# Interaction network of three layers: two sets of PSUM accumulators, one sum a period, and its transposes behind the first group of the next period

## What is computed

```python
hidden = x                                     # (512, 39, 32)
for i in range(3):
    z = jnp.einsum('bmd,bnd->bmnd', x, hidden).reshape(B, -1, D)
    cur = jnp.einsum('bcd,co->bod', z, Ws[i]) + bs[i][None, :, None]
    cur = jax.nn.relu(cur)
    if i != 2:
        hidden, direct = cur[:, :100, :], cur[:, 100:, :]
    else:
        direct = cur
    finals.append(direct)
result = jnp.sum(jnp.concatenate(finals, axis=1), axis=-1)
```

## Time and profile before

| | us |
|---|---|
| median of 3 runs | 2722.32 |
| lowest, highest | 2720.38, 2722.56 |
| profiled execution, its own time | 2722.41 |
| its span in the trace | 2720.6 |
| PE, DVE, ACT busy | 2661.5, 2642.0, 1668.8 |
| granted PE clock, mean | 0.996 |

### The profile page before, as it was taken

One profiled execution on the slowest core, in us unless ns is written; L12 is line 12 of the kernel. 1 busy time (PEld: TensorE's weight loads), 2 busy tenths in 40 slices (PEclk: granted clock), 3 DMA queues, 4 the chain that ended last, 5 costly groups with the idle time before them and its releaser, 6 DMA issues.

```text
span 2720.6 us, 52076 instructions
## 1 busy us (share of the span) xinstructions
PE 2661.5 (98%) x17960; PEld 2658.2 (98%) x17960; DVE 2642.0 (97%) x2728; ACT 1668.8 (61%) x2842; POOL 0.7 (0%) x7
## 2 busy tenths in 40 slices
PE   3899999999999999999999999999999999999999
PEld 3899999999999999999999999999999999999999
DVE  5999999999999999999999999999999999999998
ACT  3566666666666666666666666666666666666664
POOL 0000000000000000000000000000000000000000
PEclk9899999999999999999999999999999999999999
DMA  9554444444455444444544444444454444445442
GB/s 221 130 141 112 114 132 118 110 127 129 112 132 142 120 110 129 126 110 122 133 125 125 132 125 110 124 130 110 115 134 122 111 130 126 110 120 131 114 110 63
DMA packets 231026, 335.70 MB, mean 123 GB/s; under 512 B 28104, under 2 KB 165300, under 8 KB 230836
## 3 DMA queue, kind: packets, MB, share of 16 engines
q1 hardware_dynamic: 230934, 334.50, 47.2%
HBM read 329.71 MB, written 6.60 MB: 124 GB/s over the span
## 4 chain that ended last, share of the span: by engine, by line
PE 96%; DMA 1%; SPq 1%; DVE 1%; ACT 0%; issue 0%; DVEq 0%; ACTq 0%
PE acc L765 61%; PE acc L766 28%; PE acc L758 6%; PE turned L778 1%; DMA x_right<-x_by_unit 1%; DMA mixed<-in_L_rec_W_dram 0%; DMA z<-w_rows_again 0%; PE x_turned L787 0%; DVE w_split L388 0%; DVE z L430 0%; ACT w_split L650 0%; DVE z_low L435 0%; SPq L228 0%; DMA xb<-in_r_x_dram 0%; SPq L254 0%
## 5 line engine op out<-in xcount | busy, mean ns | idle before, releaser
L765 PE MATMUL acc<-w_split,z_high 128*128 128x400 f32 (+1 forms) x8320 | 2495.8, 367 | 48.1 <-DVE z_low L435 42.0
L766 PE MATMUL acc<-w_split,z_low 128*128 128x200 f32 (+1 forms) x8320 | 2121.6, 255 | 0.0
L765 PEld LDWEIGHTS acc<-w_split,z_high 128*128 128x128 f32 (+1 forms) x8320 | 1566.9, 188 | 50.6 <-issue 35.9
L766 PEld LDWEIGHTS acc<-w_split,z_low 128*128 128x128 f32 (+1 forms) x8320 | 1594.6, 192 | 0.0
L615 ACT ACTIVATE z_high<-z 128x1024 fp32r<-128x1024 f32 (+3 forms) x1152 | 1112.0, 975 | 702.0 <-DVE z L430 583.9
L435 DVE TENSOR_TENSOR z_low<-z,z_high 128x1024 fp32r<-128x1024 f32 (+3 forms) x1152 | 1281.7, 1113 | 29.6 <-PE acc L766 27.0
L430 DVE TENSOR_TENSOR z<-mixed,xb 128x1024 f32<-128x1024 f32 (+2 forms) x1024 | 1208.6, 1180 | 0.1
L640 ACT ACTIVATE mixed<-turned 32x128 f32<-32x128 f32 x768 | 204.5, 266 | 8.9
L758 PE MATMUL acc<-w_whole,z 128*128 128x200 f32 x1024 | 197.9, 337 | 1.4 <-DVE s L449 1.4
L758 PEld LDWEIGHTS acc<-w_whole,z 128*128 128x128 f32 x1024 | 169.4, 191 | 1.7 <-DVE s L449 1.7
L637 ACT ACTIVATE mixed<-turned 96x512 f32<-96x512 f32 x256 | 151.0, 590 | 11.0 <-PE turned L778 7.9
(11 more groups left out here) (29 smaller groups left out, 50.7 us busy)
## 6 DMA issues: line engine op xcount, KB each, us to landing
xb<-x_by_unit SPq DMA_DIRECT2D x384, 384.0 KB, 4.2
x_right<-x_by_unit SPq DMA_DIRECT2D x384, 136.5 KB
xb<-x_by_unit SPq DMA_DIRECT2D x384, 128.0 KB, 4.9
xb<-x_by_unit SPq DMA_DIRECT2D x128, 336.0 KB
xb<-x_by_unit SPq DMA_DIRECT2D x128, 84.0 KB
x_left<-x_by_unit SPq DMA_DIRECT2D x384, 19.5 KB
mixed<-in_L_rec_W_dram SPq DMA_DIRECT2D x4, 600.0 KB, 8.7
x_by_unit<-mixed SPq DMA_DIRECT2D x12, 160.0 KB, 2.8
```

The source lines that it names most:

```text
L765: nc.tensor.matmul(a[:, 0:2 * O], z_high[slot % HIGH_RING][0:rows, tok], w, start=(c == 0), stop=False, skip_group_check=True)
L766: last = nc.tensor.matmul(a[:, 0:O], z_low[slot % RING][0:rows, tok], w[:, 0:O], start=False, stop=(c == chunks - 1), skip_group_check=True)
```

## The change

There are now two sets of three accumulator banks; a period uses the set of its parity (`par = d % 2`), so no item writes a bank that the last period's sum still reads. With 6 banks for accumulators and one each for `turned` and `x_turned`, the turned input of a later tile goes through one bank in three parts, each part with its own wait (`turn_x`, `turned_x`), placed at three points of the period d = 4; for the first tile it uses the second set. The two half copies of a period become one of 600 columns, and the two sums one of 600, which stands behind the low part of item 2 of the next period, where `sums2` stood. `s` holds layer 2 in one row of both halves, so the addition into `direct` of 400 columns is now two of 200. `dup` and both hidden copies of ACT stand behind that sum, `dup` and the first of them behind the high part of item 3 instead of item 2. PE waits at the start of a period for the sum before the last one (`ended(n - 2)`), the wait ahead of item 5 is gone, and the transposes stand behind item 0 of the next period instead of behind item 8. `ident` has a tile of its own. At the start the second pass of layer 0 no longer waits for the first sum; at the end the last sums are cut into more pieces.

```diff
 def layers_ended(r, d):
-    return (1, 2) if r == TILES - 1 and d >= D - 2 else (0, 2)
+    if (r, d) == (0, 0):
+        return 0, 2
+    if r == TILES - 1 and d >= D - 2:
+        return 1, (2 if d == D - 1 else 3)
+    return 0, 3
...
-        acc = banks("acc", 3)
+        both = banks("acc", 6)
+        acc = [both[:, 0:3, :], both[:, 3:6, :]]
         turned = banks("turned", 1)
-        x_turned = banks("x_turned", X_BANKS)
+        x_turned = banks("x_turned", 1)
...
 # vector engine
-            def sums(a, b, step, added):
+            def sums(a, b, par, step, added):
                 dve.wait_ge(half_in, step)
                 if added is not None:
                     dve.wait_ge(direct_in, added)
-                nc.vector.tensor_tensor(s[:, a:b, :, 0:HID], acc[:, a:b, 0:O].rearrange("p l (h o) -> p l h o", o=HID),
+                nc.vector.tensor_tensor(s[:, a:b, :, 0:HID],
+                                        acc[par][:, a:b, 0:O].rearrange("p l (h o) -> p l h o", o=HID),
                                         half[:, a:b, :, :], ALU.add).then_inc(s_in, 1)
-            def sums2(u):
...
                 else:
-                    add(0, 4).then_inc(direct_in, 1)
+                    add(0, 2)
+                    add(2, 4).then_inc(direct_in, 1)
...
                 lows(base + 2, slot(2), P, group_chunks(2))
-                if not second:
-                    sums2(n - 2)
+                sums(last_a, last_b, 1 - par, ended(n - 1), n + 1)
...
                 lows(base + q + 2, slot(q + 2), P, group_chunks(2))
-                if not final:
-                    sums(a, b, ended(n), n + 2)
...
 # after the last period
             product12(2, UNITS - 1, 1, 0, at, at)
-            sums2(UNITS - 2)
+            dve.wait_ge(s_in, UNITS + 2)
+            dve.wait_ge(direct_in, UNITS + 1)
+            add(1, 2).then_inc(direct_in, 1)
             for g in range(1, GROUPS):
                 product12(2, UNITS - 1, 1, g, at + g, at + g)
+                if g == 1:
+                    sums(2, 3, 1, UNITS + 3, None)
...
 # scalar engine
                 highs(base + 2, slot(2), P, group_chunks(2))
+                second_half(last_a, last_b, 1 - par, base - 1)
                 if second:
                     high_piece(2, 2)
                     act.wait_ge(w_low_done, 8)
-                else:
-                    second_half2(base - 1)
+                highs(base + 3, slot(3), P, group_chunks(3))
+                dup(last_a, 2, ended(n - 1))
                 hidden(1, n - 1, 1 - par, ended(n - 1))
-                highs(base + 3, slot(3), P, group_chunks(3))
...
-                if not final:
+                if last_a == 0:
                     hidden(0, n + 1, 1 - par, ended(n - 1))
+                if turn:
+                    turned_x(r + 1, 0)
                 highs(base + q, slot(q), P, split_chunks(2, 0))
+                highs(base + q + 1, slot(q + 1), P, group_chunks(1))
                 if turn:
-                    for bank in range(X_BANKS):
-                        turned_x(r + 1, bank)
-                highs(base + q + 1, slot(q + 1), P, group_chunks(1))
+                    turned_x(r + 1, 1)
...
 # tensor engine
-                pe.wait_ge(s_in, ended(n - 1))
-                multiply(1, base, slot(0), 0)
-                multiply(1, base + 1, slot(1), 1)
+                pe.wait_ge(s_in, ended(n - 2))
+                multiply(1, par, base, slot(0), 0)
+                transpose(last_a, 2, ended(n - 1))
+                multiply(1, par, base + 1, slot(1), 1)
+                if turn:
+                    turn_x(r + 1, 0)
...
-                if not second:
-                    pe.wait_ge(s2_in, n - 1)
...
-                    multiply(2, base + q + g, slot(q + g), g)
-                if not final:
-                    transpose(a, b, ended(n))
+                    multiply(2, par, base + q + g, slot(q + g), g)
+                    if turn and g == 0:
+                        turn_x(r + 1, 2)
...
             at = first(UNITS)
-            pe.wait_ge(s2_in, UNITS - 1)
+            pe.wait_ge(s_in, UNITS + 1)
```

More of the change, by code:

```diff
@@ L467, in directs @@
                         fresh(0, 1)
[L468 removed]
+                    add(1, 2)
+                    add(2, 4).then_inc(direct_in, 1)
                 elif d == 1:
@@ L499, in _ @@
             low_piece(1, 1, 0)
-            sums(0, 1, 1, None)
+            sums(0, 1, 0, 1, None)
             low_piece(2, 1, 1)
@@ L512, in _ @@
             low_piece(3, 1, 2)
-            sums(0, 1, 2, 1)
+            sums(0, 1, 1, 2, 1)
             product12(1, 0, 0, 2, at + 2, at + 2)
@@ L574, in period @@
                 if final:
-                    sums(a, b, ended(n), n + 2)
+                    sums(a, b, par, ended(n), n + 2)
                 product12(2, n - 1, 1 - par, 3, base + q + 3, slot(q + 3))
                 lows(base + q + 2, slot(q + 2), P, group_chunks(2))
-                if not final:
-                    sums(a, b, ended(n), n + 2)
             for r in range(TILES):
@@ L615, in highs, with second_half @@
                 nc.scalar.activation(z_high[slot % HIGH_RING][0:rows, 0:n * T], z[0:rows, slot % RING, 0:n * T], ACT.Copy).then_inc(high, 1)
-            def second_half(a, b, last):
+            def second_half(a, b, par, last):
                 act.wait_ge(freed, RING + last + 1)
-                nc.scalar.activation(half[:, a:b, :, :], acc[:, a:b, O:2 * O].rearrange("p l (h o) -> p l h o", o=HID), ACT.Copy)\
+                nc.scalar.activation(half[:, a:b, :, :], acc[par][:, a:b, O:2 * O].rearrange("p l (h o) -> p l h o", o=HID), ACT.Copy)\
                   .then_inc(half_in, 1)
[L623 to L626, removed]
             def dup(a, b, step):
@@ L641, in hidden, with turned_x @@
                 last.then_inc(hid_in[l + 1], 1)
[L643 to L647, removed]
+            def turned_x(r, part):
+                n = min(X_PER_BANK, BLOCKS - X_PER_BANK * part)
+                act.wait_ge(x_turned_in, X_PARTS * r + part + 1)
+                nc.scalar.activation(xts(r)[:, X_PER_BANK * part:X_PER_BANK * part + n, :],
+                                     x_part(r, part)[:, 0:n * T].rearrange("p (k t) -> p k t", t=T), ACT.Copy).then_inc(xts_in, 1)
             def high_w(w, st):
@@ L654, in high_piece @@
                 high_w(piece(l, g), stage(l, g))
-            for bank in range(X_BANKS):
-                turned_x(0, bank)
+            for part in range(X_PARTS):
+                turned_x(0, part)
             act.wait_ge(pair_sum, 1)
@@ L723, in period @@
                     dup(a, b, ended(n))
-                else:
-                    second_half(a, b, base + q - 1)
                 highs(base + q + 3, slot(q + 3), P, group_chunks(3))
-                if not final:
-                    dup(a, b, ended(n))
+                if turn:
+                    turned_x(r + 1, 2)
             for r in range(TILES):
@@ L779, in transpose, with turn_x @@
                 last.then_inc(turned_in, 1)
-            def turn_x(r):
+            def turn_x(r, part):
                 pe.wait_ge(x_in, 32 * (r + 1))
                 if r > 0:
-                    pe.wait_ge(xts_in, X_BANKS * r)
-                for k in range(BLOCKS):
-                    bank, j = k // X_PER_BANK, k % X_PER_BANK
-                    t = nc.tensor.transpose(x_turned[:, bank, j * T:(j + 1) * T], x_tile(r)[:, k * P:(k + 1) * P], ident)
-                    if j == X_PER_BANK - 1 or k == BLOCKS - 1:
-                        t.then_inc(x_turned_in, 1)
+                    pe.wait_ge(xts_in, X_PARTS * r + part)
+                for k in range(X_PER_BANK * part, min(BLOCKS, X_PER_BANK * (part + 1))):
+                    j = k % X_PER_BANK
+                    last = nc.tensor.transpose(x_part(r, part)[:, j * T:(j + 1) * T], x_tile(r)[:, k * P:(k + 1) * P], ident)
+                last.then_inc(x_turned_in, 1)
             pe.wait_ge(consts, 2)
-            turn_x(0)
+            for part in range(X_PARTS):
+                turn_x(0, part)
             pe.wait_ge(w_low_done, 1)
-            multiply(0, 0, 0)
+            multiply(0, 0, 0, 0)
             transpose(0, 1, 1)
+            pe.wait_ge(xts_in, X_PARTS)
+            multiply(0, 1, 1, 1)
             pe.wait_ge(s_in, 1)
-            multiply(0, 1, 1)
             at = first(0)
```

88 lines of the change are left out of this document (42 added, 46 removed).

## The result

The changed kernel takes 2763.04 us (median of 4 runs, 2762.85 to 2763.98) where the kernel before took 2721.5 in the runs beside it: a ratio of 1.0154, with an interval of 1.0142 to 1.0166. The prediction was 2760, in a range of 2735 to 2788. The profiled execution has a span of 2761.1 us, 40.5 more than before.

The account below looks back on a forecast made before the run. PE was taken to set the pace, with DVE 0.2 us to spare a period. A new PE stall of 125 x 0.31 = 39 us, + 1 - 2, gave 2722.4 + 38 = 2760 us, range 2735 to 2788.

Parts of the forecast that it names:

- T0: The end of item 8's last matmul on PE, taken as zero of the clock of one period.
- Stop and restart: At the transposes: PE stands 0.27 us for `dup`, plus 0.04 for a slower restart, 0.31 us a period.
- the walk through the three slots: DVE's low parts followed from item 3's end through slot waits: low part 2 starts 0.19 us after item 8 ends.
- The bounds: Limits for PE's stall at the transposes: 0.08 and 0.50 us a period, with 0.31 taken.
- A: Rival: ScalarE's copies, within 0.1 us of need, delay low part and sum; 0.5 us a period, 2784 us; chance 0.15.
- The count: PE's stall at the transposes comes about 125 times: 125 x 0.31 = 39 us.
- At the start I took 2 us off: Layer 0's first pass: PE's later items stand closer to it; 2 us saved, between 0 and 3.
- The copies of the turned input: ACT's first copy ahead of item 5's high part at d = 4: 1 us for three periods, 0 to 2.7.
- At the end I had "nothing": Last sums: PE's 1.4 us wait shortened by 0.3, an extra addition costs 0.2; counted as nothing.
- The first tie: Hidden copy of layer 1 ends at 4.61, DVE wants it for item 5 at 4.58; few hundredths, no cost.
- B: Rival: path to `dup` is 0.27 us shorter, so the transposes are not late; 2721 us, no change; chance 0.08.
- C: Rival: DVE is the real pace, freeing its sums gives back 0.2 us a period; 2697 us; chance 0.05.

Follow-up runs that it names:

- early sum: Changed kernel with layers 0 and 1 summed behind the low part of item 1, layer 2 summed apart in the merged sum's place: 2718.96 us, ratio 0.9995 to the kernel before.
- exchanged sum: Changed kernel with two neighbouring VectorE instructions exchanged, the merged sum ahead of item 2's low part: 2718.51 us, ratio 0.9996 to the kernel before.

## Why the prediction was right

**The bound and the path.** The step that carried the forecast was that PE, without spare time, must wait for low part, sum, `dup` and transposes, all behind T0. It holds: when the path was shorter by 0.21 or longer by 0.13, the period followed; with `dup` over in time (early sum, exchanged sum) the loss is gone; with DVE's load cut it stays.

**Its pieces.** Predicted and measured, from T0: low part 0.19 and 0.21; sum 1.33 and 1.34, its length 0.78 and 0.78; end of `dup` 2.39 and 2.39; transposes 2.45 and 2.45. Stop and restart 0.27 + 0.04 against 0.26 + 0.05, the period 20.95 in both. That close, the walk through the three slots was worth its length: starting the low part at the lower bound, T0 + 0.11, would have given 0.23 and 29 us. The bounds were added up less well: with the pieces named there the lower one is 0.10 and not 0.08 (0.08 needs a sum of 0.68), the upper one 0.52 and not 0.50. Neither moves the range, which starts from 0.11 and ends in A.

**The count.** 125 times 0.31 is 39. The 123 steps behind the first are together 39.7 us longer; 1.7 of that is the 0.07 us at 24 loop turns, which I had not seen, and the rest is 0.31 a step. The last two of the 125 lie behind the last product of layer 0 and make 0.6 of the 2.2 us there. That the 39.0 between the first and the last product of layer 0 meet the 39 is luck: the loop turns and the short first step offset each other in part.

**The terms beside it, mostly wrong and small.** At the start I took 2 us off and 1.4 came (0.7 before the first start, 0.7 in the first step). But that is one trace against one. The kernel before and its version with the additions left out are the same up to the first start, and differ there by 1.6 us (81.89 and 80.25). So the 2 us are neither confirmed nor refuted. The copies of the turned input were to cost 1 us and cost nothing: the step at d = 4 grew by 0.29, no more than any other. At the end I had "nothing" and it was 2.2 us, 1.6 of it beyond the two usual stalls: in the last period PE comes to the transpose 1.5 us too early. The sum is late because of a wait one period earlier. That period has no layer 0, so DVE gets to the products of layer 2 sooner, and it stands 2.0 us there for the hidden copy (ACT ends it at 2710.55), which now comes behind the later transposes. The profile files the wait under "issue". From there to the sum (2727.82) DVE has no more waits:

```profile
2709.73 0.82 ACT L644 ACTIVATE mixed<-turned 32x128 f32<-32x128 f32 x3
```

```profile
2710.64 0.69 DVE L435 TENSOR_TENSOR z<-mixed,xb 128x512 f32<-128x512 f32 x1 [1.93 <-issue]
...
2727.82 0.57 DVE L452 TENSOR_TENSOR s<-acc,half 128x400 f32<-128x400 f32 x1
```

```profile
2726.90 0.25 PE L766 MATMUL acc<-w_split,z_low 128*128 128x200 f32 x1
2728.70 0.33 PE L778 MATMUL turned<-ident,s 128*128 128x128 f32 x1 [1.54 <-ACT s L634]
2728.78 0.43 PE L765 MATMUL acc<-w_split,z_high 128*128 128x400 f32 x1
```

With the early sum the end is 72.0 us again. All together, 39 - 2 + 1 = 38 us were predicted, and the traces have 40.3 - 1.4 + 1.6 = 40.5. I had looked at the steady period and at what the diff says of the end, and not at the same path in a period of other length.

**What would show it.** The step and the sum came as stated; PE's waits came in the rows of the weight loads (128 of them) and only 29 times in those of the matmuls. DVE's idle time ahead of its low parts did not come as a line: I expected 60 to 65 us, and the line for PE shows 1.5. It is there all the same, but spread over short waits, which the view of the waits leaves out and the overlap of two rows, 0.08 us, makes shorter still. In the steps from start to start, low parts of eight chunks follow products of eight by up to 1.34 and not 1.14:

```profile
1547.33 1.22 DVE L439 TENSOR_TENSOR z<-mixed,xb 128x1024 f32<-128x1024 f32 x1
1548.66 1.23 DVE L444 TENSOR_TENSOR z_low<-z,z_high 128x1024 fp32r<-128x1024 f32 x1
```

The waits of one steady period are 0.04, 0.09, 0.20 and 0.06 us ahead of four low parts, and 0.14 ahead of the products of item 5. Together that is 0.53 a period, or 66 us in 125: the 0.2 and 0.31 us that the prediction gave DVE to spare, with a quarter of it ahead of a product instead of a low part.

**The rivals.** A, ScalarE's ties: not in play, since with the copies 2.1 us later the steady period was as short as before. The first tie did fall on DVE, and by more than the few hundredths forecast: the low part of item 3 takes a step of 1.14 (1535.59 to 1536.73) where 1.00 is usual, so 0.14 us a period goes to the hidden copy, and the line with 5.4 us counts only 24 of these waits. DVE had that to spare. B needed 0.27 us less on the path, which the exchange gave. C fell with the additions left out and with the two versions that free the sums. The Trainium skill (Perfetto Trace Analysis, Optimizing Scalar/DVE Operations) has one rule for grouping where an engine is saturated and one for breaking up where it makes bubbles on another. The page gives the second for engines that are not saturated, a condition that the prediction leaves out, and DVE was busy for 97%. Still it was the breaking up that helped here: 0.21 us a period against the 0.22 that the trace had priced. The exchange shows a third way that keeps the group.

## What to carry to other kernels

Before merging or moving work of an engine that is not the bound, write down when its result is needed by the one that is, and what the new place waits for: here a sum was put behind an instruction that could not start before the very event that starts the bound engine's clock. If a chain is late by a few tenths, first look for an exchange of two neighbours in the queue; here it took away the whole loss, and cutting the sum in two in its late place only part of it. And a wait of 0.3 us that comes in every period is seen in the chain and in the steps from period to period, hardly in busy shares.

## What the runs showed of the hardware

Lengths add along a line: a sum of 200, 400 and 600 columns from PSUM took 0.36, 0.57 and 0.78 us, and the half copies 0.34, 0.50 and 0.67. From the end of one instruction to the start of the one that waited for it there were 0.03 to 0.04 us from VectorE to ScalarE, 0.05 to 0.06 from ScalarE to PE in 104 periods of the changed kernel and 0.13 in the 24 behind a loop's branch (`dup` ended at 1513.37, the transposes began at 1513.50), and about 0.1 from PE to VectorE. Not expected was that in the changed kernel a loop of eight periods costs 2.3 to 3.9 us at each jump back, where one of four costs 0.07; in the kernel before, with four, the step at a jump back is the usual 20.64.
